# Relation stage of a graph network: the further edges' rows gathered as two half rows per edge, one product for both

## The reference, cut to what matters

```
seg  = edge_type * n + dst                         # one segment per (relation, destination)
agg  = segment_sum(x[src], seg);  cnt = segment_sum(1, seg)
mean = agg / max(cnt, 1)                           # [34, 625, 768]
h1   = einsum('rni,rio->no', mean, W_rel) + x @ W_root + b
xw   = h1 @ W_gcn   ...                            # a second, dense graph convolution follows
```

## Time and profile before

| what | us |
|---|---|
| median of 3 runs (1505.83 to 1513.37) | 1510.42 |
| the profiled execution | 1503.16 |
| its span | 1501.2 |
| relation stage, about 696 to 1219 on the profile's clock | 523 |
| busy over the span: PE / DVE / ACT / POOL | 1196.0 / 883.0 / 710.7 / 636.5 |

### The profile page before, as it was taken

One profiled execution on the slowest core, in us unless ns is written; L12 is line 12 of the kernel. 1 busy time (PEld: TensorE's weight loads), 2 busy tenths in 40 slices (PEclk: granted clock), 3 DMA queues, 4 the chain that ended last, 5 costly groups with the idle time before them and its releaser, 6 DMA issues. The chain is left out here.

```text
span 1501.2 us, 31481 instructions
## 1 busy us (share of the span) xinstructions
PE 1196.0 (80%) x9690; PEld 889.0 (59%) x9691; DVE 883.0 (59%) x1741; ACT 710.7 (47%) x1048; POOL 636.5 (42%) x633
## 2 busy tenths in 40 slices
PE   8999571784676599359899999999999948863996
PEld 6776461773545477247566666666666636543775
DVE  8963568995677644363666666566666527754000
ACT  8995410764144455152464645455645423121554
POOL 0067755735541233313555555555555530021332
PEclk9999585886886699769999999999999977975998
DMA  3000210002135597565899989899999886564442
GB/s 135 1 1 4 85 18 1 2 1 84 31 106 142 186 329 264 151 243 194 242 287 274 292 258 286 244 290 268 294 274 292 241 212 182 162 134 152 79 101 52
DMA packets 115421, 247.43 MB, mean 165 GB/s; under 512 B 23566, under 2 KB 53515, under 8 KB 115345
## 3 DMA queue, kind: packets, MB, share of 16 engines
q1 hardware_dynamic: 80241, 162.83, 32.2%
q0 software_dynamic: 35104, 83.58, 23.7%
HBM read 217.06 MB, written 58.36 MB: 183 GB/s over the span
## 5 line engine op out<-in xcount | busy, mean ns | idle before, releaser
L630 PE MATMUL r_pO<-ring,r_rowsT 128*128 x2520 | 422.0, 327 | 0.0
L630 PEld LDWEIGHTS r_pO<-ring,r_rowsT 128*128 128x128 f16 x2520 | 244.0, 98 | 154.7 <-issue 1.2
L1851 DVE SCALAR_TENSOR_TENSOR ring<-q_wstage,ring 128x768 f16<-128x768 f32 x198 | 175.2, 954 | 55.6 <-ACT ring L1810 54.3
L1791 POOL DMA_INDIRECT acc_dram<-r_msg,r_scol x70 | 128.6, 1838 | 156.7 <-PE r_pT L1912 105.7
L1810 ACT ACTIVATE ring<-q_wstage 128x768 f16<-128x768 f32 x198 | 148.8, 830 | 25.9 <-issue 25.9
L1839 ACT ACTIVATE r_msg<-r_pO,slot_inv 128x768 f32<-128x768 f32 x70 | 62.7, 896 | 191.1 <-PE r_pO L630 190.9
L435 POOL DMA_INDIRECT slot_dram<-table_record,table_rowi x80 | 100.6, 1258 | 102.8 <-issue 102.1
L480 POOL DMA_INDIRECT slot_inv<-qinv_dram,slot_pair x112 | 120.0, 1072 | 49.0 <-issue 33.7
L398 PE MATMUL acc<-oh_d,oh_s 125*125 125x512 f16 (+1 forms) x800 | 134.9, 308 | 0.0
L1858 DVE TENSOR_TENSOR r_rowsT<-r_pT,r_rowsT 128x512 f16<-128x512 f32 x71 | 48.8, 688 | 101.4 <-ACT r_rowsT L1819 101.4
L1912 PE MATMUL r_pT<-r_S,q_parts 128*128 128x128 f16 x852 | 100.8, 221 | 7.8 <-DVE r_S L1868 5.1
(11 more groups left out here) (413 smaller groups left out, 2319.1 us busy)
## 6 DMA issues: line engine op xcount, KB each, us to landing
q_wstage<-in_L_gnn_W_rel_dram SPq DMA_DIRECT2D x33, 2304.0 KB, 14.2
stage<-in_L_gnn_W_dram SPq DMA_DIRECT2D x6, 768.0 KB, 7.0
wparts<-in_L_ffn_w_dram SPq DMA_DIRECT2D x8, 576.0 KB
f_stage<-in_L_ffn_w_dram SPq DMA_DIRECT2D x8, 576.0 KB, 10.8
f_stage<-in_L_ffn_w_fast_dram SPq DMA_DIRECT2D x8, 576.0 KB, 6.6
f_stage<-in_L_ffn_w_slow_dram SPq DMA_DIRECT2D x8, 576.0 KB, 7.5
f_stage<-in_L_ffn_h_fast_dram SPq DMA_DIRECT2D x8, 576.0 KB, 9.3
down_dram<-f_stage SPq DMA_DIRECT2D x8, 576.0 KB, 4.6
```

The costliest lines, as they stand in the source:

```text
L630: ins = eng.matmul(out, x, w[:, h * n:(h + 1) * n], start=first and x is xh and w is wh, stop=last and x is xl, **kw)
L1791: eng.indirect_dma_start(out=K.acc_dram[u % 2], out_offset=bass.IndirectOffsetOnAxis(ap=scol[:, u:u + 1], axis=0), in_=msg[:, u, :], in_of ...
L1851: ins_ = eng.scalar_tensor_tensor(wring[:, slot, 1, k, :], wstage[:, slot, k, :], W_SCALE, wring[:, slot, 0, k, :], ALU.mult, ALU.subtract)
```

## The change

The further edges of a relation get 64 lanes instead of 128. The second table is loaded twice, once to lanes 0 to 63 and once to lanes 64 to 127 (three DMAs at L678 and L680 instead of one). The index of a further edge is 2*src in the lower lanes and 2*src+1 in the upper, and `xn_dram` is seen as 1250 half rows of 768, so lane l holds the high half and lane l+64 the low half of the same row. S of the further edges has the same destination in both lanes, so one product sums hi and lo: `mean` has 18 products instead of 24. Relations with over 64 further edges now put them into slots. `rows[1]` is half as wide, and so is its clearing at L2057.

```diff
-                link(eng.tensor_scalar(d["fits"][:, :], total[:, 1, :], 128.0, None, ALU.is_le))
+                link(eng.tensor_scalar(d["fits"][:, :], total[:, 1, :], 64.0, None, ALU.is_le))
...
-    eng.wait_ge(loaded, 16)
+    eng.wait_ge(loaded, 48)
...
+    link(eng.tensor_scalar(K.table["part"][:, :], lane[:, :], float(N + 64), -2.0, ALU.is_ge, ALU.add))
...
-    link(eng.tensor_scalar(K.slot_idx[:, 0:T1, 1], tmp[:, :], 1.0, None, ALU.subtract))
+    link(eng.tensor_scalar(K.slot_idx[:, 0:T1, 1], tmp[:, :], 2.0, K.table["part"][:, :], ALU.mult, ALU.add))
...
-                eng.dma_start(K.table["tables"][:, :, :, :].rearrange("t a l b -> t a (l b)"),
-                              K.slot_dram.rearrange("(a t l) b -> t a (l b)", a=2, l=128)).then_inc(K.s_table_loaded, 16)
+                records = K.slot_dram.rearrange("(a t l) b -> a t l b", a=2, l=128)
+                eng.dma_start(K.table["tables"][:, 0, :, :], records[0]).then_inc(K.s_table_loaded, 16)
+                for half in range(2):
+                    eng.dma_start(K.table["tables"][:, 1, half * 64:(half + 1) * 64, :], records[1, :, 0:64, :]).then_inc(K.s_table_loaded, 16)
...
-        eng.indirect_dma_start(out=self.rows[1][:, b, :], out_offset=None, in_=self.K.xn_dram,
+        eng.indirect_dma_start(out=self.rows[1][:, b, :], out_offset=None, in_=self.K.xn_dram.rearrange("n (a c) -> (n a) c", a=2),
                                in_offset=bass.IndirectOffsetOnAxis(ap=self.gcol[:, b, 1:2], axis=0),
-                               bounds_check=N - 1, oob_is_err=False).then_inc(self.s_gathered[b], 16)
+                               bounds_check=2 * N - 1, oob_is_err=False).then_inc(self.s_gathered[b], 16)
...
-                    n = 0
-                    for side in range(2):
-                        for a in range(2):
-                            last = eng.matmul(pT[b % 2][:, k // 4, (k % 4) * 128:(k % 4 + 1) * 128], rows[side][:, b, a * C + k * 128:a * C + (k + 1) * 128],
-                                              S[:, b % 2, side, :], start=n == 0, stop=n == 3)
-                            n += 1
+                    out = pT[b % 2][:, k // 4, (k % 4) * 128:(k % 4 + 1) * 128]
+                    for a in range(2):
+                        eng.matmul(out, rows[0][:, b, a * C + k * 128:a * C + (k + 1) * 128], S[:, b % 2, 0, :], start=a == 0, stop=False)
+                    last = eng.matmul(out, rows[1][:, b, k * 128:(k + 1) * 128], S[:, b % 2, 1, :], start=False, stop=True)
...
-            rows_b = K.sb("q_rows_b", [128, UN, 2 * C], FP16, relation_ctx)
+            rows_b = K.sb("q_rows_b", [128, UN, C], FP16, relation_ctx)
```

More of the change, by code:

```diff
@@ L2141, in build @@
                 K.table = {n: K.sb("table_" + n, shape, dt, early) for n, shape, dt in (
-                    ("record", [EP, EJ, 2], FP32), ("rowi", [EP, EJ], I32), ("relf", [128, T1], FP32), ("lane", [128, 1], FP32),
+                    ("record", [EP, EJ, 2], FP32), ("rowi", [EP, EJ], I32), ("relf", [128, T1], FP32), ("lane", [128, 1], FP32), ("part", [128, 1], FP32),
                     ("tables", [T1, 2, 128, 2], FP32), ("slots", [128, 2, 2, T1], FP32), ("none", [128, 2, T1], FP32), ("tmp", [128, T1], FP32))}
```

## The result

The changed kernel took 1500.91 us, median of 12 runs (1496.83 to 1505.48), and the kernel before, beside it on the same chip, 1508.49 us (12 runs, 1505.83 to 1515.13). The ratio is 0.9945 with a 95% interval of [0.993, 0.9961], which is 8.3 us less (5.9 to 10.6). The profiled execution took 1501.56 us with a span of 1499.6.

The account below looks back on a forecast made before the run. The prediction took TensorE to bound the relation stage, with DMA close behind. Its terms, -22.1 + 13.8 + 0.2 = -8.1 us, took the median of 1510.42 us to 1502 us; own range 1496 to 1508, stretched to 1494 to 1514.

Parts of the forecast that it names:

- part 1: Mean in the relation stage: six products fewer save 0.335 us a tile; means 5 to 70 give 22.1 us, earlier ones nothing.
- The sustained spacing of about 81 ns: Skill page's price of a product: six worth 0.49 us a tile, 32 us, 1492 us; more-saved side, chance 0.09.
- The second stretch of low clock: Start of the relation stage: longer PE idle may lower the clock, costing 1.7 us or so; kept for the range.
- part 2: Relation stage: the limit of 64 makes 72 tiles from 70; two more at 6.91 us cost 13.8 us.
- part 3: Waits at turn ends and for DVE's selection matrix: seven costly turn ends against eight, taken as zero.
- part 4: Gathers, scatters and weight loads: 13.6 us of all engines a relation against PE's 13.82, taken as zero.
- The rival at 14.1 us: Transfers take over at a weight load's landing time: stage changes by -0.5 us, 1510 us; chance 0.19.
- second rival: Queue 0's gather of further edges: half rows dear at 0.29 us a packet, +12 us, 1522 us; chance 0.12.
- part 5: Outside the stage: two more table DMAs covered, one added DVE operation costs 0.2 us, halved clearing gives zero.
- the 1.4 us kept for the range: At the tables: the part of two DMAs' 4.0 us fixed cost that would show, left out of the sum.
- The 2.0 us for each DMA: Skill page's fixed cost at the two added table DMAs: 4.0 us one behind the other, left out of the sum.
- The chances: Whole-kernel outcome: faster 0.42, within 0.5% 0.46, slower 0.12; the forecast case itself had 0.60.

Follow-up runs that it names:

- run 10: The change without the product of the slots' low parts (12 products a mean, rows gathered as before), on another chip than its first try: 1485.27 us, 0.9846.
- run 3: The change with the half rows' product issued twice, so 24 products a mean and the further edges' sum counted double: 1574.54 us, 1.0058.
- run 9: The kernel before with only the limit of 64 further edges (72 tiles, 24 products, whole rows), repeated on a third chip: 1522.18 us, 1.0108.
- the limit alone: The kernel before with only 64 in place of 128 as the limit of further edges, timed twice: 1.0067 and 1.0108 of before.
- the wrapped lanes: The change with the limit at 128 again and a further edge's lane taken modulo 64 (70 tiles, 18 products): 0.9992 on one chip, 0.982 on another.
- run 5: The change itself, unaltered, on another chip: 1499.48 us, 0.994 of the kernel before.
- run 6: The change with the limit at 128 and lanes modulo 64 (70 tiles, 18 products), on another chip than its first try: 1483.31 us, 0.982.
- run 2: The kernel before with only the limit of 64 further edges (72 tiles, 24 products, whole rows), on the first, slow chip: 1575.56 us, 1.0067.
- run 11: The change lightened on PE: 12 products in the mean, 24 in the projection in place of 36, half rows gathered: 1482.38 us, 0.983.
- run 12: The kernel before with the limit of 64, lightened to 12 products in the mean and 24 in the projection, whole rows gathered: 1477.9 us, 0.9801.
- run 8: The change with limit 128 and lanes modulo 64, plus VectorE copying the gather's row numbers a step ahead: 1485.29 us, 0.9845.
- run 1: The change with the limit at 128 and lanes modulo 64 (70 tiles, 18 products), on the first, slow chip: 1565.88 us, 0.9992.
- run 4: The change without the product of the slots' low parts (12 products a mean), on the first, slow chip: 1548.83 us, 0.99.

## Why the prediction was right

The forecast was 8.1 us less than before. The measured ratio of 0.9945 makes it 8.3 less. The time of 1502 us rests on a median of 1510.42 us from three runs; from the 1508.49 of twelve it would be 1500.4, against 1500.91 measured. The mechanism held: TensorE sets the period, six products are worth 0.335 us, and two tiles come on top. That the sums agree to 0.2 us is luck, since the interval is 5 us wide, the stage alone changed by 9.0 and 10.3 us in the two profiles of the change, and small misses below cancel.

- **Six products fewer** (part 1): predicted 0.335 us a tile at the price read from the timeline, 55.8 ns each. The steady tile went from 7.25 to 6.91 us, and to 6.58 with six more gone (run 10). The sustained spacing of about 81 ns that a page states (the Trainium skill, "TensorE: Matmul & The Clock Gate", section "Back-to-back issue gap") would have given 6.76 us for the change. No tile had that.
- **The start absorbs** (part 1): I let the tiles before the stall save nothing, with PE idle for about 4.8 us before tile 5. It idled 4.53 us, and the first six steps together shrank by 0.43 us, where tiles 5 and 6 alone were to give 0.67. The second stretch of low clock, which I had left out of the sum and kept for the range, came in part: the granted clock was 0.50 until past 745 us, and the step after tile 5's idle took 1.47 us beyond the steady period where it took 1.09 before. In runs 3 and 9 the clock did not fall there and that step had no loss.
- **Two tiles more** (part 2): 72 tiles as counted. Their price, taken alone, was 10.5 and 16.3 us by the two timings of the limit alone and 14.5 and 10.9 us in their profiles, around the 14.5 of two tiles at 7.25 us. At 18 products the change and the wrapped lanes (runs 5 and 6) differ by 16 us in time and 12.8 in the stage, around the predicted 13.8.
- **Waits that move** (part 3): predicted zero. The steps from the seventh on took 4.0 us beyond the steady period before, and 3.0 and 2.1 us in the two profiles of the change. This is the one term with a small error, 1 to 2 us to the good. But the same sum ran from 2.1 to 3.8 us over five profiles with 72 tiles (runs 2, 3, 5, 9 and the changed kernel), so my count of seven costly turn ends against eight explains no more than part of it.
- **Transfers** (part 4): predicted zero, with 13.6 us of engine time per relation against PE's 13.82. Run 11 gives a floor of 13.6 us over twelve steps, and runs 10 to 12 one of 13.4 over all steps from the seventh on. The rival at 14.1 us is out, and by little: between the change and the floor lie 0.2 to 0.5 us a relation. A load's landing time of 14.1 us was not the period: in run 10 loads took 15.0 us to land at 13.4 us a pair, the next one being issued before the last had landed.
- **Half rows** (second rival): runs 3 and 11 have them at no cost. My price, a constant 0.29 us for each of 54 packets in place of 27, failed at both factors: merged lanes make 11 more packets with rows a tile and not 27, and one of 1544 bytes takes 0.07 us.
- **Outside the stage** (part 5): 0.2 us, and the two further DMAs at the tables at zero. Two profiles of the changed kernel differ by 6.4 us at the first spread, and one of them is 0.5 us behind the kernel before, so terms of this size can't be seen there. At the tables they can. The timeline of PE in the changed kernel answers to the earlier trace rows:

```profile
220.84 0.98 PE L445 MATMUL a_ps<-ident,table_tables 112*128 112x112 f32 x4
224.46 0.72 PE L908 MATMUL a_ps<-turned_rows,pick 120*128 120x125 bf16 x6 [2.64 <-DVE small L795]
```

  The tables are turned 9.2 us after the end of POOL's last scatter of records in both kernels, and PE's next work waits the same 2.64 us. The two DMAs cost nothing, and the 1.4 us kept for the range did not come. The added DVE operation shows: DVE's list of indices is complete 9.9 us after the turning begins where it was 9.7. The 2.0 us for each DMA, which the prediction named beside its sum, is stated in that section of the Trainium skill ("DMA: Bandwidth & Descriptors", "Anatomy of one DMA") for DMAs that GpSimd issues, while SP issues these.

The chances put more weight (0.46) on a result within 0.5% than on a faster one (0.42). The result, 0.55% faster, lies on that edge, and its interval reaches over both sides.

## What to carry to other kernels

Take the price of a pipelined product from start to start in the timeline, and count the tiles that a data-dependent plan makes before believing a saving per tile: here two tiles took back 14 of 22 us, and a plan that avoids them (runs 6 and 8) gives 27 and 23 us in place of 8. Before lightening the bound engine further, measure what stands behind it by a kernel in which it is lightened far too much; here that was the transfers at 13.4 to 13.6 us, 2 to 3% away. And run a tight pipeline on more than one chip: a kernel that gave 27 us on one gave nothing on another.

## What the runs showed of the hardware

**On one chip, releases came late while POOL was issuing DMAs.** There ACT started 2.6 us after the last product of the mean began, 0.07 us behind the end of POOL's issue, and a chain of four short DVE operations went in steps of 1.4 us where the others have 0.23 to 0.28. Elsewhere the same overlap did nothing: in runs 11 and 12 POOL was issuing at the end of 43 and 36 of 72 means, and no count was late. The kernel before took 1562 us there, against 1508 to 1509 us in every other set of runs. What differs about that chip no run here shows, nor how the change itself fares on it, for it wasn't run there. The page of such a profile names a false releaser (a transfer of another stage), or "issue", and only POOL's rows at the same time tell.

**Such a wait can lock.** On that chip the kernels with 24 products a tile (runs 2 and 3) lost next to nothing in the relation stage (sums of 3.9 and 3.3 us beyond the steady period), while those with 18 (run 1) and 12 (run 4) fell into alternating tiles and lost some 29 and 14 us beyond what the same kernels lost at turn ends elsewhere (sums beyond the steady period of 32.3 and 20.9 us, against 3.1 and 6.7 us in runs 6 and 10). POOL's second gather ends 1.7 us ahead of the mean's end with 24 products, 1.0 with 18 and 0.4 with 12, where releases are in time (medians of runs 9, 5 and 10). So removing work brings the gather nearer to that end, and one late count is enough to put it on top; that this starts the locking is argued from these figures and was not tested on that chip.

**Gathered half rows don't double the packets**, as run 3 shows: 11 more with rows a tile for 27 half rows more, and 1216 fewer in all on queue 0, since small ones fell.

**The HBM figure of the page counts lanes that gather nothing.** It fell from 218.63 MB with whole rows (run 2) to 203.69 MB with half rows (run 3), while queue 0 moved 84.55 and 84.54 MB. The 14.94 MB are 76 gathers by 128 lanes by 1536 bytes: the figure goes by the shape of the gather and not by what is moved, and the fall from 217.06 MB before to 203.69 MB after is no traffic saved.
